# Attention scores and row maxima on two 64-row halves of TensorE's array, in a fused attention and mixture-of-experts layer

## What is computed

```python
q = rmsnorm(x @ q_a_w.T, q_a_ln) @ q_b_w.T            # 16 heads of 64 + 64 (second part turned by rope)
ckv = x @ kv_a_w.T                                    # latent c (32) and one shared rope key (64)
kv = rmsnorm(c, kv_a_ln) @ kv_b_w.T                   # per head 64 for the keys, 128 for the values
scores = einsum('bhsd,bhtd->bhst', query, key) * scale
out = einsum('bhst,bhtd->bhsd', softmax(scores), v)
```

## Time and profile before

| | |
|---|---|
| median of 3 runs | 2381.33 us (2379.02 to 2386.78) |
| the profiled execution, its own time | 2386.19 us |
| its span, first to last instruction | 2384.4 us |
| preparation | 0 to 179.6 us |
| attention, ahead of the first scores | 179.6 to 221.4 us |
| attention, 32 half heads | 221.4 to 1723 us |
| experts and the rest | 1723 to 2384.4 us |
| one half head in steady state | 46.97 us (1030.72 to 1077.69) |

### The profile page before, as it was taken

One profiled execution on the slowest core, in us unless ns is written; L12 is line 12 of the kernel. 1 busy time (PEld: TensorE's weight loads), 2 busy tenths in 40 slices (PEclk: granted clock), 3 DMA queues, 4 the chain that ended last, 5 costly groups with the idle time before them and its releaser, 6 DMA issues. The chain is left out here.

```text
span 2384.4 us, 38677 instructions
## 1 busy us (share of the span) xinstructions
PE 2140.0 (90%) x10554; PEld 1421.9 (60%) x10554; DVE 1511.3 (63%) x3046; ACT 1375.4 (58%) x1927; POOL 1338.5 (56%) x762
## 2 busy tenths in 40 slices
PE   5896999999999999999999999999873659999990
PEld 3643666666666666666666666666553436777760
DVE  4536777777777777777777777777142324555557
ACT  2521677777777777777777777767731214555540
POOL 1001777777777777777777777777725331333330
PEclk8886999999999999999999999999986879999995
DMA  4119990000000000000000000000012244999987
GB/s 158 53 29 370 402 396 7 0 0 0 0 0 0 0 0 0 0 0 0 0 0 0 0 0 0 0 0 1 1 49 81 67 145 142 337 357 343 345 281 249
DMA packets 90336, 227.35 MB, mean 95 GB/s; under 512 B 13198, under 2 KB 46904, under 8 KB 90040
## 3 DMA queue, kind: packets, MB, share of 16 engines
q1 hardware_dynamic: 77240, 195.03, 23.1%
q0 software_dynamic: 10752, 29.72, 3.3%
q10 hardware_dynamic: 2304, 2.10, 0.3%
HBM read 125.52 MB, written 101.28 MB: 95 GB/s over the span
## 5 line engine op out<-in xcount | busy, mean ns | idle before, releaser
L632 POOL TENSOR_TENSOR prob_lo<-prob,prob_hi 128x1024 f16<-128x1024 f32 x512 | 1108.3, 2176 | 435.8 <-ACT prob_hi L651 425.8
L649 ACT ACTIVATE prob<-p_s,prob_scale 128x1024 f32<-128x1024 f32 x512 | 571.4, 1116 | 463.2 <-PE p_s L798 456.9
L684 DVE TENSOR_REDUCE maxes<-p_m 128x1 f32<-128x512 f32 x1024 | 700.7, 691 | 120.5 <-PE p_m L771 103.8
L651 ACT ACTIVATE prob_hi<-p_s,prob_scale 128x1024 f16<-128x1024 f32 x512 | 567.3, 1108 | 0.0
L771 PE MATMUL p_m<-k_hi,q_hi 96*128 96x512 f32 x1024 | 420.5, 414 | 10.4 <-DVE maxes L684 7.7
L798 PE MATMUL p_s<-q_hi,k_hi 97*128 97x512 f32 x1024 | 360.0, 433 | 5.5 <-ACT prob_hi L651 3.9
L798 PE MATMUL p_s<-q_lo,k_hi 97*128 97x512 f32 x1024 | 323.6, 397 | 0.0
L798 PE MATMUL p_s<-q_hi,k_lo 97*128 97x512 f32 x1024 | 323.1, 397 | 0.0
L1059 POOL DMA_INDIRECT ranked_out<-y,dest x128 | 122.8, 959 | 265.7 <-DVE y L1363 258.4
L771 PEld LDWEIGHTS p_m<-k_hi,q_hi 96*128 96x128 f32 x1024 | 195.4, 191 | 91.4 <-DVE maxes L684 34.8
L798 PEld LDWEIGHTS p_s<-q_hi,k_hi 97*128 97x128 f32 x1024 | 171.4, 189 | 121.2 <-issue 67.9
(11 more groups left out here) (231 smaller groups left out, 2259.0 us busy)
## 6 DMA issues: line engine op xcount, KB each, us to landing
w<-in_experts SPq DMA_DIRECT2D x128, 608.0 KB
expert_rows<-zeros SPq DMA_DIRECT2D x129, 526.0 KB, 9.1
rows<-expert_rows SPq DMA_DIRECT2D x128, 131.5 KB
got<-ranked_out SPq DMA_DIRECT2D x16, 768.0 KB, 11.1
wqb<-in_wqb SPq DMA_DIRECT2D x16, 341.0 KB, 3.0
x<-in_x SPq DMA_DIRECT2D x1, 2048.0 KB, 8.5
cbar<-in_woT SPq DMA_DIRECT2D x1, 2048.0 KB
ranked_out<-y,dest POOLq DMA_INDIRECT x128
```

The costliest lines, as they stand in the source:

```text
L632: gp.tensor_tensor(prob_lo[s % NB][:, :], prob[s % 2][:, :], prob_hi[s % NB][:, :], ALU.subtract).then_inc(lo_ready, 1)
L649: act.activation(prob[s % 2][:, :], p_s[s % 2][:, :], ACT.Exp, bias=prob_scale[:, :], scale=SCALE)
L651: act.activation(prob_hi[s % NB][:, :], p_s[s % 2][:, :], ACT.Exp, bias=prob_scale[:, :], scale=SCALE).then_inc(p_ready, 1)
L684: v.tensor_reduce(maxes[:, n:n + 1], p_m[n % 2][:, :], AX.X, ALU.max).then_inc(max_used, 1)
```

## The change

**Layout.** Keys lie twice in the array's 128 rows, once in rows 0 to 63 and once in rows 64 to 127: `kr_hi` and `kr_lo` (rope, 64 rows), `kc_pair` (latent hi in 32 rows, latent lo in the next 32) and `kc_one` (latent hi in 32 rows and a row of ones: 33). The queries of the first block of 512 columns lie in rows 0 to 63, those of the second in rows 64 to 127: `qr_hi`, `qr_lo`, `qc_hi` (the latent part twice), `qc_lo` (with the negated maxima in row 32 of each half).

**Scores.** Five rounds per key tile instead of three parts: in each round two matmuls of up to 64x512, one per half of the rows, each into its own bank of p_s. A group has 20 slots.

**Maxima.** 16 instead of 32 for a half head; each is two rounds of two matmuls into both banks of p_m, which is now one buffer of 128x1024, and one VectorE reduction of 128x1024 to 128x2. They stand at slots 1, 5, 9, 13, 17 of groups 0 and 2 and at 1, 4, 7, 11, 14, 17 of group 1.

**Projection.** Both query blocks at once on two halves of the output partitions: `project_rope` behind the slots of group 1, `project_rest` behind those of group 2, and on VectorE the split into hi and lo at the end of the half head, after it has seen the last scores of the half head that used those buffers. One `rows` at slot 7 of group 3. VectorE's steps in it are marked and waited for once (`mark`, `settle`).

**Preparation.** GpSimd makes the key tensors from `kraw` (10 operations for each of four blocks); VectorE clears two tiles; the normalisation of the queries (`rq`) goes into hT instead of cosq and sinq; some tiles share memory.

```diff
-STEPS_V = 4 * 4 + 2
-MX = 2 * T
+STEPS_V = 2 * 8
+MX = T
...
+            for q in range(T // 4):                       # gpsimd, preparation
...
+                gp.wait_ge(kraw_ready, q + 1)
+                for part in (turned, slice(rest, rest + ROPE)):
+                    gp.tensor_copy(kr_hi[part, cols], kraw[turned, :]).then_inc(hi_ready, 1)
+                for b in range(2):
+                    for tile in (kc_one, kc_pair):
+                        gp.tensor_copy(tile[b * ROPE:b * ROPE + C, cols], kraw[kept, :]).then_inc(hi_ready, 1)
+                gp.wait_ge(hi_ready, 6 * q + 6)
+                for part in (turned, slice(rest, rest + ROPE)):
+                    step(gp.tensor_tensor(kr_lo[part, cols], kraw[turned, :], kr_hi[turned, cols].bitcast(F32), ALU.subtract))
...
-        p_m = [pb("p_m0"), pb("p_m1")]
+        p_m = pb("p_m", 2 * QC)
...
-            at = [[] for _ in range(12)]
-            begin, end, done = {0: (2, 11, 0), 1: (1, 12, 9), 2: (0, 12, 20), 3: (0, 0, 32)}[g]
+        PARTS = ((kr_hi, qr_hi, ROPE), (kr_hi, qr_lo, ROPE), (kr_lo, qr_hi, ROPE), (kc_pair, qc_hi, 2 * C),
+                 (kc_one, qc_lo, KR))
+        SLOTS = 4 * len(PARTS)
...
+                for i, slot in enumerate(((1, 5, 9, 13, 17), (1, 4, 7, 11, 14, 17), (1, 5, 9, 13, 17), ())[g]):
+                    at[slot].append(("max", (0, 5, 11, 16)[g] + i))
             if g == 0 and not first:
-                at[2].append(("turn", 0))
-            if g == 0 and more:
-                at[11].append(("project", 1))
+                at[9].append(("turn", None))
             if g == 3 and more:
-                at[1].append(("row", 0))
-                at[3].append(("row", 1))
-            if g == 3 and after:
-                at[5].append(("project", 0))
+                at[7].append(("rows", None))
...
+            def project_rope(m, half, use):               # vector
...
+                step.mark(v.tensor_tensor(qr_raw[:, :], p_x[:, :], cosq[:, tok], ALU.mult))
+                for n, (dst, src) in enumerate(((HALF, 0), (0, HALF), (ROPE + HALF, ROPE), (ROPE, ROPE + HALF))):
+                    turned = v.tensor_tensor(rot[dst:dst + HALF, :], p_x[src:src + HALF, :], sinq[src:src + HALF, tok], ALU.mult)
+                    if n < 3:
+                        step.mark(turned)
+                turned.then_inc(x_used, 1)
...
+                step(v.tensor_tensor(qr_raw[:, :], qr_raw[:, :], rot[:, :], ALU.add))
+            def project_rest(m, use):
+                v.wait_ge(x_mm, use + 1)
+                v.tensor_copy(qc_raw[:, :], p_x[:, :]).then_inc(x_used, 1)
...
+            def split(m, half, first=False):
+                if not first:
+                    v.wait_ge(s_mm, 16 * m - 16)
+                step(v.tensor_copy(qr_hi[half][:, :], qr_raw[:, :]))
+                v.tensor_copy(qc_hi[half][:, :], qc_raw[:, :]).then_inc(q_ready, 1)
+                step(v.tensor_tensor(qr_lo[half][:, :], qr_raw[:, :], qr_hi[half][:, :].bitcast(F32), ALU.subtract))
...
             def maximum(n, m):
                 v.wait_ge(max_mm, MX * m + n + 1)
-                v.tensor_reduce(maxes[:, n:n + 1], p_m[n % 2][:, :], AX.X, ALU.max).then_inc(max_used, 1)
+                v.tensor_reduce(by_tile[:, n // 4, :, n % 4], p_m[:, :].rearrange("p (c n) -> p c n", c=2), AX.X,
+                                ALU.max).then_inc(max_used, 1)
...
-            for s, n in ((x_used, 1), (q_ready, 1), (max_used, 2), (p_ready, 2), (lo_ready, 2), (o_mm, NB), (o_copied, 1)):
+            for s, n in ((x_used, 1), (max_used, 1), (p_ready, 2), (lo_ready, 2), (o_mm, NB), (o_copied, 1)):
...
                 pe.wait_ge(max_used, MX * m + n + 1)      # tensor, maximum
-                pe.matmul(p_m[n % 2][:, :], q_hi[half][0:KA, j * P:(j + 1) * P], k_hi[0:KA, kc * QC:(kc + 1) * QC],
-                          start=True, stop=True).then_inc(max_mm, 1)
+                for part, (kk, qq) in enumerate(((kr_hi, qr_hi), (kc_pair, qc_hi))):
+                    for c in range(2):
+                        b = slice(c * ROPE, (c + 1) * ROPE)
+                        last = pe.matmul(p_m[:, c * QC:(c + 1) * QC], qq[half][b, j * P:(j + 1) * P],
+                                         kk[b, kc * QC:(kc + 1) * QC], start=(part == 0), stop=(part == 1))
+                last.then_inc(max_mm, 1)
...
+                kk, qq, n = PARTS[part]                   # tensor, scores
+                for c in range(2):
+                    b = slice(c * ROPE, c * ROPE + n)
+                    last = pe.matmul(p_s[kt % 2][:, c * QC:(c + 1) * QC], kk[b, kt * P:(kt + 1) * P], qq[half][b, :],
+                                     start=(part == 0), stop=(part == len(PARTS) - 1))
```

More of the change, by code:

```diff
@@ L482, in _ @@
             pe.wait_ge(fold_ready, 32)
-            with pe.Fori(0, T // 4) as q:
+            for q in range(T // 4):
                 pe.wait_ge(k_ready, 12 * q + 12)
@@ L714, in half_head @@
                         copy_out(m - 1)
-                    for todo in plan(g, first, more, after):
-                        for what in todo:
-                            kind, c = what
-                            if kind == "max":
-                                maximum(c, m + 1)
-                            elif kind == "turn":
-                                turn(1 - half, h - (1 - half), x_use(m, what) - (0 if more else 1))
-                            elif kind == "row":
-                                row(c, 1 - half, x_use(m, what))
-                            elif c == 1:
-                                project(m + 1, 1, 1 - half, x_use(m, what))
-                            else:
-                                project(m + 2, 0, half, x_use(m, what))
+                    for todo in plan(g, first, more):
+                        for what, n in todo:
+                            if what == "max":
+                                maximum(n, m + 1)
+                            elif what == "turn":
+                                turn(1 - half, h - (1 - half), x_use(m, what) - (0 if more else missing))
+                            else:
+                                rows(m + 1, 1 - half, x_use(m, what) - missing)
+                    if g == 1 and after:
+                        project_rope(m + 2, half, x_use(m, "rope"))
+                    if g == 2 and after:
+                        project_rest(m + 2, x_use(m, "rest"))
+                if after:
+                    split(m + 2, half)
             step(v.tensor_copy(identr[:, :], ident[:, :]))
-            for c in range(2):
-                project(0, c, 0, c)
+            project_rope(0, 0, 0)
+            project_rest(0, 1)
+            split(0, 0, first=True)
             for n in range(MX):
                 maximum(n, 0)
-            for c in range(2):
-                row(c, 0, 2 + c)
-            project(1, 0, 1, 4)
+            rows(0, 0, 2)
+            project_rope(1, 1, 3)
+            project_rest(1, 4)
+            split(1, 1, first=True)
             half_head(0, 0, first=True)
@@ L817, in half_head @@
                 m = 2 * h + half
+                missing = 0 if after else 2
                 for g in range(4):
-                    at = plan(g, first, more, after)
-                    for slot in range(12):
-                        kt, part = 4 * g + 2 + slot // 3, slot % 3
+                    at = plan(g, first, more)
+                    for slot in range(SLOTS):
+                        kt, part = 4 * g + 2 + slot // len(PARTS), slot % len(PARTS)
                         if kt < 16:
```

261 lines of the change are left out of this document (144 added, 117 removed).

## The result

The changed kernel takes 2739.68 us (median of 4 runs, 2733.71 to 2752.81); the kernel before took 2383.45 in the same comparison. The ratio is 1.150, with a 95% interval of 1.146 to 1.155. The prediction was slower, 2595 us, within 2520 to 2715: the direction is right, the time is 25 us beyond the upper end.

What follows compares the result with a forecast made beforehand. The prediction took TensorE to bound the kernel. 31 half heads, each 6.3 us longer at 53.25, gave +195 us, and +18 outside the loop gave 2599 in the profiled execution, so 2595 median, range 2520 to 2715.

Steps and rivals of the forecast that it cites:

- Row halves run side by side: Scores and maxima on TensorE: both matmuls of a round run together, 0.232 us a round; 16 rounds, 3.7 us, fall away.
- The chain of 2.03 us: From one maximum's start to the next through VectorE's reduction: 2.03 us, stretching 13 intervals in a half head.
- Groups 1, 2 and 3: Parts of a half head in the loop: forecast at 16.05, 14.9 and 9.9 us, against 11.48, 11.44 and 10.81 before.
- the projections side by side: Query projections on column halves in groups 1 and 2: costed as before, two of 1.72 us.
- group 3's bound by p_s: Last group of a half head: two p_s buffers and ScalarE hold it at 9.9 us, against 7.8 of TensorE's work.
- Group 0: First group of a half head: forecast at 12.4 us, against 13.24 before, which has a projection in it.
- Outside the loop: Work ahead of the loop, the last half head and the preparation: together +18 us.
- The sixteen-fold chain: Maxima ahead of the loop at half clock, nothing to hide them: 16 times 2.52 us, 40.3 us, +15.
- Staging of the second block: Ahead of the loop: two stages share p_x with VectorE's rope between, split before the first maximum; estimated +4 us.
- B: Rival for TensorE's rounds: row halves run one after the other, +20.4 us a half head, about 3045 us; chance 0.11.
- D: Rival for the projections: column halves run one after the other, +102 us, 2697 us; chance 0.07.
- C: Rival for the maxima: fully hidden, -108 us, about 2280; decided at a reduction of 0.7 us; chance 0.08.

Runs made afterwards that it cites:

- before_joined: The kernel before with only p_m made one buffer of two banks, 16 maxima with one reduction of 1024 columns each; 2532.63 us, ratio 1.1037.
- late_split: The kernel after with split's two subtractions moved to the ends of groups 0 and 2 of the next half head; 2525.56 us, ratio 1.0995.
- small_gpsimd: The kernel after with GpSimd subtracting only 64 of the 1024 columns of each prob_lo tile, order of operations unchanged; 2521.45 us.
- late_half_reduction: late_split with each maxima reduction over only 256 of the 512 columns of both banks, output not the reference's; 2317.55 us.
- late_spread: late_split with one maximum moved from group 1 to slot 1 of group 3, and rows to slot 10; 2542.49 us, ratio 1.1048.

## Why the prediction was right and where it failed

- **Row halves run side by side: right.** Both matmuls of a round start together, and rounds lie 0.23 apart. The 0.30 us that I had estimated from the Trainium skill's factor for four row tiles ("TensorE: Matmul & The Clock Gate", Part 3: Packing small matmuls) is not what two tiles of 64 rows cost here. TensorE around two maxima of the kernel after:

```profile
1099.52 0.50 PE L842 MATMUL p_m<-kr_hi,qr_hi 64*128 64x512 f32 x2 [1.19 <-DVE maxes L735]
1099.86 0.40 PE L842 MATMUL p_m<-kc_pair,qc_hi 64*128 64x512 f32 x2
1100.10 0.39 PE L872 MATMUL p_s<-qr_lo,kr_hi 64*128 64x512 f32 x2
...
1101.58 0.50 PE L842 MATMUL p_m<-kr_hi,qr_hi 64*128 64x512 f32 x2 [0.40 <-DVE maxes L735]
```

- **The chain of 2.03 us: right.** It is 2.05, here and in `before_joined`, and it is the mechanism of most of the loss. The waits in the half head shown of the kernel after have, for the earlier trace rows (total us, times, longest):

```profile
PEld p_m L842 <- DVE maxes L735: 14.4, 12, 3.9
```

  About 10 was forecast; in a half head of `late_split` it is 11.6.
- **Groups 1, 2 and 3: right** within 0.3 us, and with them the projections side by side (eight matmuls from 1106.83 to the sums at 1108.59, 1.76 us; 1.72 forecast) and group 3's bound by p_s.
- **Group 0: the step that failed.** The sentence is "`split` lies beside it on VectorE, 0.9 us up to `q_ready`; its two subtractions have all the rest of the group." I gave it undisturbed durations and a group to hide in. It begins only behind the last scores of the old buffers and `rows`, 5.6 us before the group's end, and takes 9.3 beside GpSimd instead of 2.2. The part up to `q_ready` alone takes 4.3 instead of 0.9, which is still in time; it is the subtractions behind it that hold VectorE. My own sum had group 0 begin with VectorE free. The measured half head is 4.5 us over the forecast, 4.3 of them in group 0; 31 times 4.5 is 141, and the loop's 337.6 less the forecast 193 is 145. Both the duration (VectorE's work at its undisturbed length) and the overlap (nothing queued behind it) were wrong, and the lower clock behind the wait was no term of the sum. `late_split` and `small_gpsimd` each give 129 of it back and land on the forecast half head (53.74 against 53.25).
- **The trace of before had rows for it.** In the earlier trace rows the addition of two operands in SBUF lasts 0.99 us for 64x512, where the undisturbed one of 128x512 is 0.69; GpSimd ended a run of three operations at 1044.05, 0.54 before it was done. And in the same half head the subtraction that makes `q_lo` lasts, as VectorE's groups of the kernel before show,

```profile
L679 DVE TENSOR_TENSOR q_lo<-q_raw,q_hi 96x512 fp32r<-96x512 f32 x3 | 5.7, 1897 | 0.1
```

  1897 ns in the mean of three, 0.69 us where GpSimd is idle (1045.09). I took 0.99 for a dearer operation and didn't look at the other row. The Trainium skill ("SBUF — State Buffer", Who interferes with whom) says that VectorE's casts in a two-port mode, and its operations with two SBUF inputs, share a port pair with GpSimd by an exclusive lock held for the whole instruction. The trace agrees: 0.43 becomes 2.0 to 2.3 beside GpSimd operations of 2.1 to 2.3, and reads of PSUM stay at 0.69 and 1.22.
- **Outside the loop: +18 against +20** (the forecast +18 less its -2, which lies in the loop). That it is so close is in part luck, since the parts are off and offset each other. The sixteen-fold chain ran from 197.48 to 238.10, 40.6 us (40.3 forecast). Staging of the second block cost nothing (I had 4), and one `rows` instead of two `row` behind the chain gave 2.3 back (I had nothing). The preparation cost +4.9 (I had 1); the last 36 products of it begin at 164.85 where they began at 160.09, so the delay came earlier, and I did not follow it.
- **Rivals.** B is out (rounds of 0.23), D is out (1.76 us). C's turning point, a reduction of 0.7 us, is where `late_half_reduction` met the kernel before; its prize was half of what I gave it, 53 us instead of 108.

## What to carry to other kernels

When two buffers are made into one larger one, the producer and the consumer take turns: work out the whole turn (both sides' work, both handovers, the restart) and compare it with the work that the producer has between two of them, before counting the instructions that the merger saves. An elementwise operation of VectorE that reads and writes SBUF is to be costed at the duration that it has beside GpSimd, and placed where nothing queues behind it. A long stall of TensorE can cost more than itself: here one of 3.5 us was followed by 3.4 us or more at the lower clock.

## What was not expected of the hardware

- Casts with one input (128x512, fp32 to fp32r) are held up by GpSimd as much as subtractions with two: 0.43 to 2.0 and 2.25 us, and 0.69 to 2.4 and 2.6. Reductions and copies from PSUM are not.
- After a gap of 3.9 us between the starts of two matmuls TensorE ran at 1.2 GHz for 3.4 us (granted clock 0.90 in the group). In `late_spread` it ran at 1.2 GHz for 6.8 us after waits of 1.13 and 0.84 us close together, but only in every second half head, though the others have nearly the same waits. In `late_split`, with twelve waits for the maxima of 0.4 to 1.2 us in a half head, every group of that half head has a granted clock of 1.00.
- A half-height matmul of a maximum and one of a score, with different weights, operands and banks, start together as the two of one round do.
